# Expert-choice gathers: GpSimd waits for landed rows after every second batch instead of after each

## The chip, the cores and the metric

The kernel runs on one NeuronCore of a Trainium2 chip. The metric is the device time of one launch in microseconds (us), as the median of several runs. One further execution was taken with the hardware profiler; all rows below come from it.

## The reference

The program is an audio tower on 16 sequences of 750 steps: a convolution with batch norm, a linear-attention layer, an expert-choice mixture of experts, a cross-attention to video, and a top-2 mixture of experts. The change touches the third of these alone:

```python
affinity = softmax(einsum('bsd,de->bse', x, gate_weight)).transpose(0, 2, 1)
gating, index = top_k(affinity, k)                     # k = 92 tokens for each of 16 experts
x_in = take_along_axis(x[:, None], index[..., None], axis=2)
h = gelu(einsum('bekd,edh->bekh', x_in, w1) + b1)
x_e = einsum('bekh,ehd->bekd', h, w2) + b2
out = zeros_like(x).at[batch, index].add(gating[..., None] * x_e)
```

Each expert picks its 92 tokens of each sequence; their rows (128 numbers) are gathered, run through the expert's two layers, weighted and added back at the tokens they came from.

## The kernel before

The stage is `expert_choice_phase`. The 16 sequences are taken as 8 pairs (called p0 to p7 here). A pair has 2 x 16 x 92 picked rows, which are 23 tiles of 128 rows. The tiles are gathered in 6 batches (g0 to g5) of 4, 4, 4, 4, 4 and 3 tiles; a batch holds two tiles of each of the pair's sequences, in the order in which the experts need them.

GpSimd gathers (L1226 to L1241). For each tile it issues one indirect DMA (L1237) that reads 128 rows of `xs` in HBM, at the row numbers in a column of `rowu`, into one slot of `xg`. There is a slot for every tile of a pair, so batch g of pair p needs only that batch g of pair p-1 has been transposed (`t_ps`, L1233). Behind each batch GpSimd waits until all of its tiles have landed (L1241); each batch has a semaphore `got[g]` of its own. Before p0 and before p4 GpSimd also makes the row numbers for the next four pairs (`rows_of`, L1216), from a table `place` that ScalarE copies out of PSUM (L1289).

TensorE, ScalarE and VectorE follow one list of units that is written out ahead (`ExpertOrder.units`, L993). A unit "gathered" of batch g waits on `got[g]`, transposes its tiles on TensorE (L1389), and ScalarE copies them to `xgT` (L1301, L1303). "hidden" and "output" are the two matmuls of an expert (L1396, L1404) with ScalarE's activation behind each (L1311, L1320). "turned" transposes results back and splits them in a high part (ScalarE, L1330) and a low part (VectorE, L1183), and VectorE builds selection matrices (L1191). "spread" multiplies them into the token sums (L1428), "added" adds a sequence's sums to `h` (L1444, L1202). The front units of pair p+1 (gathered, hidden, output) are woven between the spread units of pair p, so that in p0 only front units run, and after that both kinds run together. One unit "rows" in the middle of p2's spreads (L1015) turns the lists for p4 to p7 into the table `place`.

While p0 to p2 run, VectorE also picks the tokens of the last eight sequences (L1155 to L1159).

Of the kernel before, what the change touches and what calls it, by code (L numbers as in the profile page):

```python
# [1021 lines left out]
def expert_choice_phase(nc, k):  # L1022

    stack, sb, sem = phase_scope(nc, k)
    with stack:
        F32R = mybir.dt.float32r
        HB = B // 2
        order = ExpertOrder()
# [39 lines left out]
        got = [sem(f"got{g}") for g in range(order.BATCHES)]  # L1068
# [14 lines left out]
        def column(p, tile):  # L1083
            return p * TILES + tile
# [4 lines left out]
        with nc.Block() as block:  # L1089
            @block.sync  # L1090
            def _(sp):
                sp.dma_start(base[:], k.expert_base).then_inc(tables, 16)
                sp.dma_start(iota[:], k.token_iota.partition_broadcast(P)).then_inc(tables, 16)
                for i in range(PAIRS):
                    for g in range(4):
                        b = i * 2 + g // 2
                        sp.wait_ge(nt.normed, i * 4 + (g + 1))
                        if g % 2 == 0:
                            sp.dma_start(xs_b[b, 0:GW, :].rearrange("(j p) d -> p j d", p=P),
                                         nt.xl[:, g]).then_inc(kept[g], 16)  # L1100
                        else:
                            sp.dma_start(xs_b[b, GW:GW + 2 * P, :].rearrange("(j p) d -> p j d", p=P),
                                         nt.xl[:, g, 0:2, :]).then_inc(kept[g], 16)
                            sp.dma_start(xs_b[b, T - LAST:T, :], nt.xl[0:LAST, g, 2, :]).then_inc(kept[g], 16)
                for hf in range(2):
                    sp.wait_ge(packed, hf + 1)
                    sp.dma_start(k.lists[hf].rearrange("a (p k) -> p a k", k=CAP),
                                 pack[:, hf, :, 0:CAP]).then_inc(listed_out[hf], 16)
                    sp.wait_ge(listed_out[hf], 16)
                    if hf:  # L1110
                        sp.wait_ge(row_ps, hf)
                    sp.dma_start(listed[:], k.lists[hf].rearrange("a (t s) -> t a s", s=P)).then_inc(listed_in[hf], 16)
# [101 lines left out]
            @block.gpsimd  # L1214
            def _(pool):
                def rows_of(hf):  # L1216
                    pool.wait_ge(row_moved, hf + 1)
                    if hf == 0:
                        pool.wait_ge(tables, 32)
                    nc.gpsimd.tensor_tensor(rowf[:, :], place[:, hf * HT:(hf + 1) * HT],  # L1220
                                            base[:, hf * HT:(hf + 1) * HT], ALU.add).then_inc(row_ready, 1)
                    pool.wait_ge(row_ready, 2 * hf + 1)
                    nc.gpsimd.tensor_copy(rowu[:, hf * HT:(hf + 1) * HT], rowf[:, :]).then_inc(row_ready, 1)
                    pool.wait_ge(row_ready, 2 * hf + 2)

                for p in range(PAIRS):  # L1226
                    if p % HP == 0:
                        for g in range(4):
                            pool.wait_ge(kept[g], 16 * (1 + g % 2) * (p + HP))
                        rows_of(p // HP)  # L1230
                    for g in range(order.BATCHES):
                        if p:
                            pool.wait_ge(t_ps, (p - 1) * order.BATCHES + g + 1)  # L1233
                        lows, highs = order.batch[g]
                        for j, tile in enumerate(lows + highs):
                            col = column(p, tile)
                            nc.gpsimd.indirect_dma_start(  # L1237
                                out=xg[:, 4 * g + j, :], out_offset=None, in_=k.xs,
                                in_offset=bass.IndirectOffsetOnAxis(ap=rowu[:, col:col + 1], axis=0),
                            ).then_inc(got[g], 16)  # L1240
                        pool.wait_ge(got[g], 16 * order.count(g) * (p + 1))  # L1241

            @block.scalar
            def _(act):
# [1139 lines left out]
```

## Time and profile before

| What | us |
|---|---|
| runs | 2298.33, 2295.48, 2301.55 |
| median of the runs | 2298.33 |
| the profiled execution's own time | 2295.3 |
| span of its instructions | 2293.4 |
| first gather issued (L1237) | 669.9 |
| last gather issued (L1237) | 986.1 |
| last addition to `h` in this stage (L1207) | 1033.4 |

Times in the rows are us from the start of the span; durations marked ns are not. PE is TensorE's matmuls, PEld its weight loads (which run ahead of the matmuls by a little), DVE is VectorE, ACT is ScalarE, POOL is GpSimd. A bracket at a row's end is the time that the engine was idle before it, and what released it; "issue" means that nothing in the profile shows what it waited for. PEclk is the granted TensorE clock, 1.00 being 2.4 GHz and 0.50 being 1.2 GHz.

### The profile page before, as it was taken

The page shows a single profiled execution, that of the slowest core. Times are in us where ns is not written, and L with a number is a line of the kernel's source. Part 1 is how long each engine was busy: PE and PEld are TensorE (multiplying, and loading weights), DVE is VectorE, ACT ScalarE, POOL GpSimd, SP SyncE. Part 2 cuts the span into 40 slices and gives each one's busy share as a digit, 9 for nine tenths or more (in the row PEclk, how much of TensorE's full clock was granted, in tenths as well). Part 3 has the DMA queues.
Part 4 walks back from the last instruction along what each step waited for, and adds up shares of the span by engine and source line. Part 5 has one row for each costly group of instructions (what it writes and reads, how often), then busy time and mean ns, then how long its engine had stood idle before and what let it go on. Part 6 is the DMA issues. An engine that isn't in the chain of part 4 may idle for free. (4 is left out here: it accounts for less than half of the span.)

```text
span 2293.4 us, 54841 instructions
## 1 busy us (share of the span) xinstructions
PE 2042.9 (89%) x20986; PEld 1801.0 (79%) x20986; DVE 1628.5 (71%) x4183; ACT 1075.9 (47%) x2698; POOL 608.5 (27%) x650
## 2 busy tenths in 40 slices
PE   6699999989747888986999999985999999999998
PEld 5488777778536878874777777775999999999998
DVE  4755556554583855665999999987777777777773
ACT  4433333332344555644666666642444444444443
POOL 0002222220025555511333333333212221221220
PEclk9799999999868999998999999997999999999999
DMA  8100000100211111100000000000000000000000
GB/s 184 42 1 12 11 11 11 15 8 1 76 56 40 42 34 40 41 10 2 3 3 3 3 3 3 3 2 1 8 8 14 7 7 14 7 7 14 7 8 14
DMA packets 80356, 44.52 MB, mean 19 GB/s; under 512 B 45800, under 2 KB 74024, under 8 KB 79752
## 3 DMA queue, kind: packets, MB, share of 16 engines
q1 hardware_dynamic: 74248, 29.53, 5.7%
q0 software_dynamic: 5888, 12.07, 2.0%
q8 instruction: 137, 2.24, 0.4%
q14 instruction: 83, 0.68, 0.1%
HBM read 27.20 MB, written 14.38 MB: 18 GB/s over the span
## 5 line engine op out<-in xcount | busy, mean ns | idle before, releaser
L2105 ACT ACTIVATE w<-banks,b 128x384 f32<-128x384 f32 (+1 forms) x512 | 259.7, 573 | 393.0 <-PE banks L2179 393.0
L2161 PE MATMUL banks<-w,w 128*128 128x128 f32 (+1 forms) x3072 | 364.1, 275 | 0.0
L2161 PEld LDWEIGHTS banks<-w,w 128*128 128x128 f32 (+1 forms) x3072 | 350.4, 189 | 9.1 <-issue 8.7
L1689 PE MATMUL banks<-qT,w 64*64 64x128 f32 x4608 | 272.2, 271 | 3.2 <-ACT eb L1641 2.4
L1697 PE MATMUL banks<-eb,w 64*64 64x128 f32 x4608 | 272.4, 271 | 0.2 <-DVE eb L1596 0.2
L1689 PEld LDWEIGHTS banks<-qT,w 64*64 64x64 f32 x4608 | 249.3, 133 | 16.6 <-DVE eb L1596 2.2
L1661 POOL TENSOR_TENSOR t<-eb 128x768 f32<-128x768 f32 x96 | 174.6, 1819 | 309.2 <-ACT eb L1641 299.3
L1697 PEld LDWEIGHTS banks<-eb,w 64*64 64x64 f32 x4608 | 249.2, 133 | 0.9 <-DVE eb L1596 0.8
L2002 DVE SCALAR_TENSOR_TENSOR h<-banks,t_wt,h 128x128 f32 (+3 forms) x672 | 183.8, 344 | 83.1 <-PE banks L2161 79.7
L1237 POOL DMA_INDIRECT xg<-xs,rowu x184 | 179.5, 976 | 127.0 <-DMA xg<-xs,rowu 84.7
L1596 DVE TENSOR_TENSOR eb<-eb,rd 128x1536 f32<-128x1536 f32 x96 | 208.6, 2172 | 2.1 <-ACT rd L1650 2.1
L2177 PE MATMUL banks<-t_xh,t_w1h 128*128 128x384 f32 (+1 forms) x512 | 182.5, 356 | 0.1
L1592 DVE TENSOR_REDUCE nm<-banks 128x128 bf16<-128x1536 f32 x96 | 167.8, 1748 | 10.8 <-PE banks L1689 10.8
L2179 PE MATMUL banks<-t_xh,t_w1l 128*128 128x384 f32 (+1 forms) x512 | 171.7, 335 | 0.0
L2178 PE MATMUL banks<-t_xlo,t_w1h 128*128 128x384 f32 (+1 forms) x512 | 171.0, 334 | 0.0
L2045 POOL TENSOR_TENSOR t_rstd<-t_nv,t_minus_half 128x6 f32<-128x6 f32 x48 | 63.6, 1326 | 399.7 <-DVE t_nv L1903 398.3
L1641 ACT ACTIVATE eb<-banks 128x512 f32<-128x512 f32 x288 | 150.5, 598 | 0.0
L1183 DVE SCALAR_TENSOR_TENSOR x_yl<-banks,gates,x_yh 128x128 fp32r<-128x128 f32 x184 | 52.0, 345 | 129.3 <-ACT x_yh L1330 129.1
L1428 PE MATMUL banks<-x_sel,x_yh 128*128 128x374 f32 (+1 forms) x384 | 119.7, 393 | 2.1 <-ACT x_oT L1339 1.9
L1191 DVE TENSOR_SCALAR x_sel<-iota,place 128x748 fp32r<-128x748 f32 x184 | 104.6, 622 | 6.3 <-PE banks L1428 6.2
L729 ACT ACTIVATE DT<-banks 128x768 f32<-128x768 f32 x60 | 48.7, 811 | 123.6 <-PE banks L822 123.6
L1428 PE MATMUL banks<-x_sel,x_yl 128*128 128x374 f32 (+1 forms) x384 | 98.8, 339 | 0.0
(300 smaller groups left out, 4325.3 us busy)
## 6 DMA issues: line engine op xcount, KB each, us to landing
out<-h SPq DMA_DIRECT2D x16, 320.0 KB
xs<-r_xl SPq DMA_DIRECT2D x16, 192.0 KB, 2.8
h<-in_xT SPq DMA_DIRECT2D x4, 750.0 KB, 14.8
h<-in_xT SPq DMA_DIRECT2D x4, 749.0 KB, 17.6
xg<-xs,rowu POOLq DMA_INDIRECT x184
xs<-r_xl SPq DMA_DIRECT2D x16, 128.0 KB
blocks<-NT SPq DMA_DIRECT2D x24, 48.0 KB, 1.9
D<-blocks SPq DMA_DIRECT2D x24, 48.0 KB, 2.1
```

What stands on the lines that cost most here:

```text
L1237: nc.gpsimd.indirect_dma_start(out=xg[:, 4 * g + j, :], out_offset=None, in_=k.xs, in_offset=bass.IndirectOffsetOnAxis(ap=rowu[:, col:col ...
L1428: last = nc.tensor.matmul(k.ps[:, 5 + s, 0:TW // 2], y[lo:hi, col % 8, :], sel[lo:hi, col % SEL, s * (TW // 2):(s + 1) * (TW // 2)], start ...
L1596: nc.vector.tensor_tensor(eb[:, w % 4], eb[:, w % 4], rd[:, w % 2, None, :].to_broadcast([P, FR, P]), ALU.mult).then_inc(w_ready, 1)
L1661: nc.gpsimd.tensor_tensor(t1[:, n % 2], e[:, 0:6], e[:, 6:12], ALU.add).then_inc(tree, 1)
L1689: last = nc.tensor.matmul(lbanks(n)[place(n, hd), v, :], k.Kt[half(hd), v, :], qT[half(hd), n // NC % 2, (n % NC) * P:(n % NC + 1) * P], s ...
L1697: last = nc.tensor.matmul(k.ps[half(hd), 6, 0:P], k.Vd[place(a, hd), v, half(hd)], eb[place(a, hd), a % 4, v, :], start=(v == 0), stop=(v ...
L2002: last = nc.vector.scalar_tensor_tensor(out=hh, in0=k.psf[0:n, o:o + P], scalar=wt[0:n, par, c * E1 + e:c * E1 + e + 1], in1=hh if e else ...
L2105: nc.scalar.activation(gb[u % 2][:, f, s * GW:s * GW + NFREE[s]], k.ps[:, order.bank(n), 0:NFREE[s]], ACT.Relu, bias=k.b1_1[:, 2 * e + f:2 ...
L2161: last = nc.tensor.matmul(k.psf[0:n, o:o + P], gb[u % 2][:, f, c * P:c * P + n], k.w2_1[:, 2 * e + f, :], start=(f == 0), stop=(f == 1))
L2177: nc.tensor.matmul(ps, w1h[:, 2 * e + f, :], xh[:, g, 0:w], start=True, stop=False)
L2178: nc.tensor.matmul(ps, w1h[:, 2 * e + f, :], xlo[:, g, 0:w], start=False, stop=False)
L2179: nc.tensor.matmul(ps, w1l[:, 2 * e + f, :], xh[:, g, 0:w], start=False, stop=True).then_inc(full, 1)
```

## The change

The wait of L1241 stands behind the odd batches alone, and there it waits for the even batch before it and then for the odd one. Nothing else is changed.

```diff
@@ -1238,7 +1238,9 @@
                                 out=xg[:, 4 * g + j, :], out_offset=None, in_=k.xs,
                                 in_offset=bass.IndirectOffsetOnAxis(ap=rowu[:, col:col + 1], axis=0),
                             ).then_inc(got[g], 16)
-                        pool.wait_ge(got[g], 16 * order.count(g) * (p + 1))
+                        if g % 2:
+                            for done in (g - 1, g):
+                                pool.wait_ge(got[done], 16 * order.count(done) * (p + 1))
```

On GpSimd's own program, the gathers of p0 stand like this before (`got0` to `got5` are the landings of the six batches, `row_ready` the row numbers, `g_t_ps` the transposes that free a slot):

```order
L1237 DMA xg<-xs,rowu 128x128 [waits row_ready]
L1237 DMA xg<-xs,rowu 128x128 x3
L1237 DMA xg<-xs,rowu 128x128 [waits got0]
L1237 DMA xg<-xs,rowu 128x128 x3
L1237 DMA xg<-xs,rowu 128x128 [waits got1]
L1237 DMA xg<-xs,rowu 128x128 x3
L1237 DMA xg<-xs,rowu 128x128 [waits got2]
L1237 DMA xg<-xs,rowu 128x128 x3
L1237 DMA xg<-xs,rowu 128x128 [waits got3]
L1237 DMA xg<-xs,rowu 128x128 x3
```

A wait is shown on the instruction that follows it. In the changed kernel the same place on GpSimd, and the first batches of p1 behind it, read:

```order
L1237 DMA xg<-xs,rowu 128x128 [waits row_ready]
L1237 DMA xg<-xs,rowu 128x128 x7
L1237 DMA xg<-xs,rowu 128x128 [waits got1,got0]
L1237 DMA xg<-xs,rowu 128x128 x7
L1237 DMA xg<-xs,rowu 128x128 [waits got3,got2]
L1237 DMA xg<-xs,rowu 128x128 x6
L1237 DMA xg<-xs,rowu 128x128 [waits g_t_ps,got5,got4]
L1237 DMA xg<-xs,rowu 128x128 x3
L1237 DMA xg<-xs,rowu 128x128 [waits g_t_ps]
L1237 DMA xg<-xs,rowu 128x128 x3
L1237 DMA xg<-xs,rowu 128x128 [waits g_t_ps,got1,got0]
```

The gathers are issued in runs of 8, 8 and 7 instead of 4, 4, 4, 4, 4 and 3. From p1 on, the wait for a free slot (`g_t_ps`) stays ahead of every batch. The order of instructions on the other engines is the same as before.

## Rows read from the trace of the kernel before

**Rows 1.** Waits by line, 669 to 990 us: us in total, times, longest.

```profile
POOL xg L1237 <- DMA xg<-xs,rowu: 84.7, 46, 2.4
POOL xg L1237 <- issue: 41.6, 136, 0.4
PE banks L1389 <- DMA xg<-xs,rowu: 34.5, 15, 6.7
```

**Rows 2.** Timeline of POOL: start us, us, instruction, [idle before it, releaser].

```profile
669.88 1.20 POOL L1237 DMA_INDIRECT xg<-xs,rowu  x1 [0.30 <-POOL rowu L1223]
...
676.59 0.94 POOL L1237 DMA_INDIRECT xg<-xs,rowu  x1 [1.76 <-DMA xg<-xs,rowu]
...
708.57 0.94 POOL L1237 DMA_INDIRECT xg<-xs,rowu  x1 [1.81 <-DMA xg<-xs,rowu]
...
822.67 0.94 POOL L1237 DMA_INDIRECT xg<-xs,rowu  x1 [0.31 <-issue]
833.29 0.84 POOL L1220 TENSOR_TENSOR rowf<-place,x_base 128x92 f32<-128x92 f32 x1 [9.67 <-ACT place L1289]
...
834.89 0.98 POOL L1237 DMA_INDIRECT xg<-xs,rowu  x1 [0.43 <-POOL rowu L1223]
```

**Rows 3.** Busy time by stretch: us, PE, PEld, DVE, ACT, POOL, PEclk, DMA share, GB/s.

```profile
669.00:708.50 39.50, 17.52 (x60) 12.82 (x59) 14.84 (x26) 12.34 (x32) 22.51 (x25) 0.59 0.15 39
873.50:912.00 38.50, 35.25 (x220) 32.14 (x219) 24.13 (x64) 23.61 (x70) 22.28 (x23) 1.00 0.16 40
```

**Rows 4.** Timeline of PE, transposes of gathered batches (L1389), p0, p1 and p4.

```profile
703.10 1.12 PE L1389 MATMUL banks<-ident,xg 128*128 128x128 f32 x4 [2.25 <-DMA xg<-xs,rowu]
...
720.15 0.60 PE L1389 MATMUL banks<-ident,xg 128*128 128x128 f32 x4
721.74 0.63 PE L1389 MATMUL banks<-ident,xg 128*128 128x128 f32 x4 [0.30 <-DMA xg<-xs,rowu]
728.22 1.11 PE L1389 MATMUL banks<-ident,xg 128*128 128x128 f32 x4 [3.45 <-DMA xg<-xs,rowu]
...
741.36 0.66 PE L1389 MATMUL banks<-ident,xg 128*128 128x128 f32 x4 [0.74 <-DMA xg<-xs,rowu]
...
847.93 1.11 PE L1389 MATMUL banks<-ident,xg 128*128 128x128 f32 x4 [4.75 <-DMA xg<-xs,rowu]
...
854.50 0.66 PE L1389 MATMUL banks<-ident,xg 128*128 128x128 f32 x4 [1.23 <-DMA xg<-xs,rowu]
...
861.35 0.66 PE L1389 MATMUL banks<-ident,xg 128*128 128x128 f32 x4 [2.10 <-DMA xg<-xs,rowu]
867.93 0.66 PE L1389 MATMUL banks<-ident,xg 128*128 128x128 f32 x4 [0.86 <-DMA xg<-xs,rowu]
```

**Rows 5.** Timeline of PEld, weight loads of g4's transposes (812.98: g3), p2 to p7.

```profile
780.53 0.42 PEld L1389 LDWEIGHTS banks<-ident,xg 128*128 128x128 f32 x4 [0.26 <-DMA xg<-xs,rowu]
...
812.98 0.42 PEld L1389 LDWEIGHTS banks<-ident,xg 128*128 128x128 f32 x4 [0.72 <-DMA xg<-xs,rowu]
819.95 0.42 PEld L1389 LDWEIGHTS banks<-ident,xg 128*128 128x128 f32 x4 [1.55 <-DMA xg<-xs,rowu]
...
906.40 0.42 PEld L1389 LDWEIGHTS banks<-ident,xg 128*128 128x128 f32 x4 [0.40 <-DMA xg<-xs,rowu]
...
944.79 0.42 PEld L1389 LDWEIGHTS banks<-ident,xg 128*128 128x128 f32 x4 [0.33 <-DMA xg<-xs,rowu]
...
983.34 0.42 PEld L1389 LDWEIGHTS banks<-ident,xg 128*128 128x128 f32 x4 [0.52 <-DMA xg<-xs,rowu]
```

**Rows 6.** Stretches around p1's third batch and p4's second: as Rows 3.

```profile
730.00:735.00 5.00, 5.00 (x23) 4.97 (x22) 2.99 (x9) 2.68 (x9) 2.59 (x4) 0.65 0.21 56
...
845.00:850.00 5.00, 2.07 (x8) 2.08 (x9) 0.44 (x1) 0.92 (x3) 2.58 (x4) 0.62 0.15 39
```

**Rows 7.** Durations of gathers and selections: ns min/median/max, first and last start.

```profile
L1237 POOL DMA_INDIRECT xg<-xs,rowu x184: 942/947/1340, 669.9 to 986.1; - x184
L1191 DVE TENSOR_SCALAR x_sel<-iota,place x184: 584/603/815, 709.4 to 1026.9; 128x748 fp32r<-128x748 f32 x184
```

## The prediction

> **What bounds the stage now.** I read the waits first. In this stage GpSimd is held 46 times until a batch has landed, 84.7 us in all, so 1.84 us a time; between two gathers of one batch it loses 41.6/136 = 0.31 us [rows 1]. With the bare 0.947 us of a gather [rows 7], a batch of four takes some 5 us to issue and 1.5 us more until the next begins. The waits follow each other without a pause in which GpSimd is idle for another reason, but for the change of tables at 823.6 to 834.9 us [rows 2]: GpSimd paces itself.
>
> The second view is the timeline: does anyone need the rows that soon? From the first gather of p0 (669.88) to the first of p1 (708.57) GpSimd takes 38.7 us a pair [rows 2]. TensorE is held 15 times, 34.5 us in all, by rows that have not landed [rows 1], and the reader should see where. In p0 TensorE has only front units to do and is busy 17.5 of 39.5 us at a mean clock of 0.59; in p5 it is busy 35.3 of 38.5 us at full clock [rows 3]. So the gathers bound the ramp plainly, and the steady part seems bound by TensorE. But the weight loads show that even there batch g4 is met exactly as it lands, in every pair from p2 on, with waits of 0.26 to 1.55 us [rows 5]. GpSimd's pace and TensorE's own are within half a microsecond of each other per pair. The question is therefore not how much GpSimd saves, but how far TensorE can go ahead before its own pace binds.
>
> **What one removed wait is worth on GpSimd.** Behind an even batch the 1.84 us wait becomes an ordinary gap of 0.31 us: 1.53 us each, three in a pair, 4.6 us of 38.7, 24 in all, so 36.8 us of GpSimd's time. The wait that stays should cost what it does now: the even batch was issued some 5 us before and has landed, so the first of the two waits passes at once. I take the landing itself as unchanged, because the wait behind the last batch of p0, which has three gathers, is 1.81 us, and behind the first, which has four, 1.76 us [rows 2]: nothing piles up. At one gather per 1.25 us, and landed some 1.5 us after its issue, no more than two are in flight, with the wait or without.
>
> So a batch lands earlier by 1.53 us for each even batch between it and the last fixed start. The fixed starts are 669.88 (p0) and, for p4 to p7, the table `place`.
>
> **p0 and p1.** Batch g4 of p0 has two fewer waits ahead of it: TensorE transposes it at 703.10 - 3.06 = 700.04. From there to g0 of p1 it waits for no rows, 17.05 us (703.10 to 720.15 [rows 4]); so 717.1. For g1 it was held 0.30 us and will not be: 718.4. It is ready for g2 3.03 us later (728.22 - 3.45 - 721.74), at 721.4; g2 now has four fewer waits ahead and lands at 728.22 - 6.1 = 722.1. TensorE is still held, by 0.7 us instead of 3.45. From g2 to g4 it needs 741.36 - 0.74 - 728.22 = 12.40 us, part of it at the lowered clock that followed the 3.45 us pause (0.65 in 730 to 735 [rows 6]); without the pause some 1 us less, my estimate from that clock over half of those 5 us. So it is ready for g4 at 733.5 to 734.5, and g4 lands at 741.36 - 5 x 1.53 = 733.7. The gain up to here is 6.9 to 7.65 us; I take **7.3**. The landing caps it: if TensorE's clock rose sooner in p0, it would meet g2 and g4 of p1 at the same times.
>
> **p2 and p3.** Here GpSimd is ahead for good (at g4 of p3, 11 waits or 16.8 us earlier against TensorE's 9). What is left to gain is the waits for rows that end: 0.26, 0.72 and 1.55 us on the weight loads [rows 5], 2.5 us; on the matmuls less shows, so **2.2**. From then on TensorE runs at its own pace, and GpSimd's saving buys nothing.
>
> **The change of tables.** GpSimd finishes p3 12 waits (18.4 us) earlier, but `place` comes from the unit "rows" on TensorE, which moves only by 9.5 us. The idle time ahead of L1220, 9.67 us [rows 2], grows to some 18.6 us: the larger part of what GpSimd saved in p0 to p3 becomes this wait. No other engine waits on GpSimd here.
>
> **p4.** Gathers start anew from the table, and TensorE has nothing left to run ahead of. It was held 4.75 us for g1, 1.23 for g2, 2.10 for g3, 0.86 for g4 [rows 4]. Counted from the table, g1 and g2 land 1.53 us earlier, g3 and g4 3.06. Between the batches TensorE needs 5.34, 4.75 and 5.72 us (start to start, less the waits). So g2 would be ready at 847.93 - 1.53 + 5.34 = 851.74 and lands at 852.97; g3 is ready at 857.72 and lands at 858.29; g4 is ready at 864.01 and lands at 864.87. It is held to the end by rows, so g4 gains the whole **3.06**. If the clock stays low longer (0.62 in 845 to 850 [rows 6]), less: with 1 us more between g3 and g4, 2.9.
>
> **p5 to p7.** With GpSimd ahead again, the waits for g4 end: 0.40 + 0.33 + 0.52 = **1.25 us** [rows 5]. Slots are no limit: at the first gather of p7 GpSimd is ahead by 9 more waits, 13.8 us, on a lead of nearly a pair.
>
> **Sum.** 7.3 + 2.2 + 3.06 + 1.25 = 13.8 us. The profiled execution takes 2295.3 us, of which 1.9 lies around the span; it would take 2281.5. The median of the runs is 2298.33, 3.0 above it, and they spread over 6 us; I carry the gain over to the median: **2284.5 us**. What follows the stage starts when its last addition is done and moves with it. The bounds of the terms (6.9 to 7.65, 1.7 to 2.5, 2.0 to 3.06, 0 to 1.25) give 10.6 to 14.5 us, 2283.8 to 2287.7; with the spread of the runs, 3 us to each side, about 2280.5 to 2291.
>
> **A rule that speaks against it.** The rows say that a gather takes 947 ns as a median, 1340 at most, while VectorE makes 184 selections of 603 ns beside them, and a pair's 23 gathers take 22.3 us on GpSimd against a bare 23 x 0.947 = 21.8 [rows 3, 7]: at most half a microsecond a pair is lost to whatever VectorE does. The Trainium skill, page "SBUF — State Buffer", section "SBUF: two separate sides", says that while VectorE runs a fast-mode operation GpSimd is locked out of their common port and cannot write a DMA's descriptors. By that rule alone each selection could hold a gather for its whole 603 ns, 13.9 us a pair as an estimate, three times what the change saves; the trace shows half a microsecond, and I go by the trace.
>
> **The rivals.**
>
> *TensorE's own pace binds sooner.* Only the waits of the two ramps count: g4 of p0 gains 3.06 us, and p4 gains 3.06; in p1 the chain of ScalarE and TensorE, or a clock that comes up later, takes the rest. For it: p5 looks full (35.3 busy of 38.5 [rows 3]). Against it: TensorE is idle 3.45 us for g2 of p1 [rows 4], and that wait has four fewer ahead of it. 6.1 us, 2292.2 us: no change by the measure below. Chance 0.11.
>
> *An even batch lands only with the odd one behind it.* Then the gathers between two waits act as one: g4 of p0 comes with g5, three gathers of 1.25 us later, at 703.8 instead of 700.04, later than now; g4 of p1 at 733.7 + 3.75 = 737.5, a gain of 3.9; p2 and p3 still give 2.2; in p4, g4 comes at 864.87 + 3.75 = 868.6 and loses 0.7. That leaves 5.4 us: 2292.9. The equal waits behind three and four gathers speak against it [rows 2]. Chance 0.05.
>
> *Slower: gathers stretch.* Denser gathers meet VectorE's selections more often, and each is issued more slowly. The point from which this decides is 4.6/23 = 0.2 us a gather, a mean of 1.15 us. The longest seen is 1.340 us [rows 7], 0.39 above the median: 9.0 us a pair if all were like that, 4.4 worse than now, and over 8 pairs 35 us, 2333 us. It would strike all pairs, since GpSimd would again set the pace of each. Half a microsecond a pair now speaks against it. Chance 0.05. The page named above stands behind this rival.
>
> **How the numbers follow.** The forecast has 0.79. A difference of over 0.3%, 6.9 us here, is about what a measurement of this kernel tells from no change: faster means below 2291.4. The forecast's range lies there, but a draw of runs can take 0.01 of it out, and the first rival's 2292.2 can fall on either side (0.03 of its 0.11): 0.81 faster. Same: 0.08 of the first rival, the second's 0.05 and the forecast's 0.01, 0.14. Slower: the third, 0.05. The range for 8 in 10 goes from 2279 to 2293, to take in the first rival.
>
> **What would show it.** Right: 22 waits of some 1.84 us ahead of gathers on GpSimd instead of 46; g4 of p1 transposed near 734 and never met at its landing from p2 to p3 and from p5 on; the wait ahead of the second L1220 near 18.6 us; TensorE's waits for rows down from 34.5 us to about 23, nearly all in p0 and p4. Wrong: gathers with a mean above 1.1 us, waits for rows in p5 to p7, or a wait of 3 us or more left at g2 of p1.

## The result, and the profile after

The changed kernel takes 2337.64 us in the median, the kernel before 2297.49 in the runs beside it: a ratio of 1.0178, 95% interval 1.0161 to 1.0195. Slower by 40 us; the forecast was 2284.5. The profiled execution's span is 2335.6 us.

Where does the time go? The first gather is issued at 669.81, as before; the last addition to `h` of this stage comes at 1075.3 instead of 1033.4. So nearly the whole loss, 41.9 us of the 42.2 between the two profiled spans, arises in this stage. I look first at what the forecast spoke of. GpSimd's timeline in the changed kernel (start us, us, instruction, idle before it and releaser):

```profile
669.81 1.20 POOL L1237 DMA_INDIRECT xg<-xs,rowu  x1 [0.30 <-POOL rowu L1223]
...
682.11 0.94 POOL L1237 DMA_INDIRECT xg<-xs,rowu  x1 [2.37 <-DMA xg<-xs,rowu]
...
694.01 0.94 POOL L1237 DMA_INDIRECT xg<-xs,rowu  x1 [2.23 <-issue]
...
704.76 0.94 POOL L1237 DMA_INDIRECT xg<-xs,rowu  x1 [2.33 <-issue]
...
847.70 0.37 POOL L1220 TENSOR_TENSOR rowf<-place,x_base 128x92 f32<-128x92 f32 x1 [37.22 <-ACT place L1291]
```

Against [rows 2] p0 is issued in 34.9 us instead of 38.7: GpSimd did get ahead. Each wait that stays is 2.2 to 2.4 us instead of 1.84. And the wait for the table `place` is 37.2 us, where 18.6 was forecast. The page's group of gathers and TensorE's transposes (the same view as [rows 4]) say that the rows came early:

```profile
L1237 POOL DMA_INDIRECT xg<-xs,rowu x184 | 179.1, 973 | 114.6 <-issue 86.3
```

```profile
700.43 0.95 PE L1391 MATMUL banks<-ident,xg 128*128 128x128 f32 x4 [2.07 <-DMA xg<-xs,rowu]
706.54 0.49 PE L1391 MATMUL banks<-ident,xg 128*128 128x128 f32 x3
721.38 1.05 PE L1391 MATMUL banks<-ident,xg 128*128 128x128 f32 x4
723.48 1.05 PE L1391 MATMUL banks<-ident,xg 128*128 128x128 f32 x4
728.19 0.60 PE L1391 MATMUL banks<-ident,xg 128*128 128x128 f32 x4
732.42 0.60 PE L1391 MATMUL banks<-ident,xg 128*128 128x128 f32 x4
740.90 0.60 PE L1391 MATMUL banks<-ident,xg 128*128 128x128 f32 x4
```

A gather's issue has a mean of 973 ns: nothing stretched. Batch g4 of p0 is transposed at 700.43 (forecast 700.04). But p1 begins at 721.38, later than the 720.15 of before, and from there to p4 TensorE waits for rows no more: it is late by itself. Seven of the waits of 669 to 1005 us (us in total, times, longest) name the new cause:

```profile
ACT x_yT L1322 <- remote: 20.9, 9, 5.3
PE banks L1406 <- ACT x_yT L1322: 19.8, 12, 4.9
POOL xg L1237 <- PE banks L1391: 20.5, 5, 12.2
ACT hid L1313 <- remote: 18.9, 10, 4.1
PE banks L1391 <- DMA xg<-xs,rowu: 17.6, 6, 7.1
PE banks L1398 <- ACT hid L1313: 13.1, 11, 2.4
DVE x_sel L1191 <- remote: 8.4, 5, 2.4
```

TensorE's row waits fell from 34.5 us [rows 1] to 17.6. "Remote" is new: before has no such wait in the stage. Here ScalarE is held by a semaphore of TensorE whose matmul had long ended by the profile. One place in p1, first ScalarE, then TensorE, then GpSimd beside them:

```profile
786.93 0.41 ACT L1322 ACTIVATE x_yT<-banks,b 128x184 f32<-128x184 f32 x1 [3.21 <-remote]
```

```profile
781.09 0.48 PE L1406 MATMUL banks<-hid,w 128*128 128x184 f32 x2
...
782.12 0.47 PE L1398 MATMUL banks<-xgT,w 128*128 128x184 f32 x2
787.49 0.95 PE L1406 MATMUL banks<-hid,w 128*128 128x184 f32 x2 [4.90 <-ACT x_yT L1322]
```

```profile
775.48 0.94 POOL L1237 DMA_INDIRECT xg<-xs,rowu  x1 [2.35 <-PE banks L1391]
...
784.22 0.94 POOL L1237 DMA_INDIRECT xg<-xs,rowu  x1 [0.30 <-issue]
787.40 1.01 POOL L1237 DMA_INDIRECT xg<-xs,rowu  x1 [2.24 <-issue]
```

The output matmul (L1406) ends at 781.57, and TensorE goes on to others; ScalarE, which needs its result, starts at 786.93. A semaphore update is the mark that a finished instruction sets for the engines that wait for it; the trace holds the times of these events. They tell what came between (time of the event, and how long after the end of the latest matmul that can have made it):

```
782.56  TensorE L1416   2.59
785.42  TensorE L1430   3.14
786.87  TensorE L1446   5.61
786.91  TensorE L1406   5.34
786.97  TensorE L1430   4.69
787.01  TensorE L1398   4.42
```

Four updates of TensorE come out within 0.15 us, in the break between a run of eight gathers and the next. A matmul's end is modelled in these profiles (the Trainium skill, page "Perfetto Trace Analysis", section "Tensor Engine Instruction (MATMUL, LD_WEIGHTS)", says so too), but an error of the model would not end for four matmuls at once. I call an update late when it comes over 0.4 us after the latest matmul that makes it. Of the events that the trace holds from 690 to 1000 us (it lacks some: 465 stand there for 531 matmuls that make one in before, 373 for 445 in the changed kernel), 36 of TensorE's 465 are late in before, 25.6 us in all; in the changed kernel 111 of 373, 225.7 us. VectorE and ScalarE have none late in either, and after the last gather TensorE has none either.

What late updates cost shows where TensorE does the same work. The next rows (columns as in [rows 3]) go from the last batch's transposes of one pair to those of the next: first before, p1 to p2, then the changed kernel, p1 to p2 and p2 to p3.

```profile
748.91:788.10 39.19, 35.22 (x219) 32.20 (x218) 33.99 (x85) 23.38 (x69) 22.73 (x24) 1.00 0.16 42
```

```profile
748.86:805.87 57.01, 41.52 (x219) 37.68 (x218) 34.47 (x85) 23.59 (x71) 34.84 (x37) 0.88 0.18 47
805.87:841.92 36.05, 34.51 (x219) 32.24 (x218) 23.27 (x65) 23.42 (x70) 3.24 (x3) 1.00 0.03 7
```

The same 219 matmuls take 57.0 us instead of 39.2 while GpSimd is at work on 37 gathers beside them, and 30 of the 57 updates on record are late. TensorE is idle 11.5 us more, and its matmuls take 6.3 us more at a mean clock of 0.88 instead of 1.00. In the next stretch GpSimd issues its last gathers before the table and then waits for it (3 instead of 37 fall in the stretch); no update is late, and TensorE needs 36.05 us, less than before's 39.4 for that pair. Up to the last batch of p1 the two kernels are level (748.86 and 748.91); the loss arises in p2 (17.8 us), p5 (19.4) and p6 (12.6). In p3 and p7, with 3 gathers each in these stretches, it gains 3.4 and 2.8 on before, and in p4, where TensorE has rows to wait for, 1.7.

### The profile page after: what moved, and what is told of

The parts are those of the page before. It is cut to its first block and busy times, and to the rows that moved or that the text cites. A ratio compares the mean times of both kernels' runs of the same rounds, so it can differ in the third digit from the quotient of the medians.

```text
span 2335.6 us, 54823 instructions
## 1 busy us (share of the span) xinstructions
PE 2064.0 (88%) x20986; PEld 1819.6 (78%) x20986; DVE 1628.5 (70%) x4183; ACT 1075.2 (46%) x2698; POOL 607.2 (26%) x650
## 5 line engine op out<-in xcount | busy, mean ns | idle before, releaser
L1430 PE MATMUL banks<-x_sel,x_yh 128*128 128x374 f32 (+1 forms) x384 | 125.0, 408 | 3.7 <-ACT x_oT L1341 2.9
L1191 DVE TENSOR_SCALAR x_sel<-iota,place 128x748 fp32r<-128x748 f32 x184 | 105.3, 622 | 19.4 <-PE banks L1430 11.0
L1430 PE MATMUL banks<-x_sel,x_yl 128*128 128x374 f32 (+1 forms) x384 | 104.3, 355 | 0.0
```

The source lines that it names most:

```text
L1430: last = nc.tensor.matmul(k.ps[:, 5 + s, 0:TW // 2], y[lo:hi, col % 8, :], sel[lo:hi, col % SEL, s * (TW // 2):(s + 1) * (TW // 2)], start ...
```

## The experiments

The theory: TensorE's semaphore updates are held up while GpSimd issues gathers closely, and the longer the run, the longer. Rivals: it is the landing that must be awaited; the second wait instruction costs the time; the bytes or the rows of the gathers do it; TensorE's updates are too many. Unless a diff shows more, it replaces the wait of L1241, `pool.wait_ge(got[g], ...)`. "Landed" stands for that line. `pause(n)` is n memsets on GpSimd, each waited for:

```diff
+        idle, idled = sb("x_idle", [P, 400]), sem("x_idled")
...
+                def pause(times):
+                    for _ in range(times):
+                        nc.gpsimd.memset(idle[:], 0.0).then_inc(idled, 1)
+                        pauses[0] += 1
+                        pool.wait_ge(idled, pauses[0])
```

### A pause in place of the landing

```diff
+                        if g % 2:
+                            wait for landed g - 1, then g
+                        else:
+                            pause(3)
```

> The changed kernel, but behind each even batch GpSimd clears a scratch tile three times (some 1.5 us by its other clears) without waiting for any row. Theory 'pause': TensorE's semaphore updates queue up while GpSimd issues gathers back to back, from the fourth in a row on, and any stretch without a gather lets them through; then runs of four come back and the time returns to that of before, 2290 to 2303 us. Theory 'landing': the updates queue until GpSimd has waited for its rows, so that what counts is the number of gathers since the last such wait; then the time stays at 2330 to 2345 us, as in the changed kernel (2337.6).

Measured: 2309.19 us, ratio 1.0053 (1.0034 to 1.0072); 41 of 411 late. Nothing is awaited behind an even batch, and 28 of the 40 us are back. The time lies above the 2290 to 2303 expected; the rest goes with GpSimd's pace, whose runs of four start 6.94 us apart (median of p0 to p3) instead of 6.61. e8 below has the same 6.94 and takes 2307.15 us.

### Runs of twelve

```diff
+                        if g % 3 == 2:
+                            wait for landed g - 2, g - 1, then g
```

> The wait stands behind every third batch (12 and 11 gathers in a row). If the loss grows with the length of the run (both theories above): TensorE's updates come later still, and the time lies above the changed kernel's 2337.6, at 2345 to 2380 us. Rival, a fixed price of having more than one batch in flight: within 5 us of 2337.6, 2333 to 2343.

Measured: 2356.22 us, ratio 1.0263 (1.0236 to 1.0290); 86 of 342 late, 276.6 us. The loss grows with the run.

### The second wait instruction, alone and left out

Before with one wait more (e8), and the change with one wait less (e9):

```diff
 e8
+                        wait for landed g - 1 (odd g only), then g
 e9
+                        if g % 2:
+                            wait for landed g
```

> Before, with one more wait for the even batch's rows ahead of the odd batch's own, which are long satisfied when GpSimd comes to it. Theory (a second wait instruction costs GpSimd some 0.4 us, as the odd waits of 2.2 to 2.4 us against 1.84 suggest): three such waits a pair, 1.2 us a pair and up to 9.6 us in all where GpSimd paces; with TensorE's own pace in p2, p3 and p5 to p7 part of it hidden: 2300 to 2307 us. Rival (a satisfied wait is free, the longer wait comes from the eight gathers): 2297 us, odd waits of 1.84 us.

> The changed kernel with only the odd batch's own wait behind it: runs of eight gathers, one wait. Theory that the loss comes from the runs of eight: 2328 to 2338 us, late updates of TensorE as in the changed kernel, odd waits near 1.84 us. Rival that the second wait brings a large part of the loss: under 2315 us.

Measured: e8 2307.15 us, ratio 1.0046 (1.0029 to 1.0062); e9 2340.43, ratio 1.0193 (1.0176 to 1.0210). Two rows of GpSimd's timeline in e8, behind the first even and the first odd batch:

```profile
677.10 0.94 POOL L1237 DMA_INDIRECT xg<-xs,rowu  x1 [1.70 <-DMA xg<-xs,rowu]
...
684.05 0.95 POOL L1237 DMA_INDIRECT xg<-xs,rowu  x1 [2.25 <-DMA xg<-xs,rowu]
```

A wait that is already satisfied is not free on GpSimd: 0.55 us here, 0.48 between the medians of the odd and the even batches. 24 of them are 13 us at most, and e8 is 10 us slower: most of it shows in the time, so in before a delay of GpSimd is passed on nearly whole. But in the changed kernel this is not the loss: e9 without it is as slow.

### The change in p0 alone

```diff
+                        if g % 2 or p:
+                            wait for landed g - 1 (odd g only), then g
```

> The even waits are gone in the first pair alone, where TensorE has little to do and is held by the rows themselves; all other pairs wait behind each batch as before. By the prediction's own terms this first pair gives 3 to 4.6 us; where the late updates cost as much there as elsewhere (40 us over 8 pairs, 5 a pair), it is lost again. Theory 'late updates': 2293 to 2303, no gain beyond 3 us. Rival, the prediction's sum holds where GpSimd is the bound: 2290 to 2294.

Measured: 2301.27 us, ratio 1.0024 (1.0009 to 1.0040). This edit puts the second wait into every pair, so it is to be read against e8, which has it too: p0's earlier rows are worth 5.9 us.

### A short pause behind each batch, and one twice as long

```diff
 e4, memset of 400 elements
+                        pause(1)
 e6, memsets of 300 elements
+                        pause(2)
```

> No wait for landed rows on GpSimd at all; behind each batch of four it clears a scratch tile once (some 0.45 us, with the gaps around it 0.8 us without a gather instead of 1.84). Theory 'pause', if the queued updates drain in well under a microsecond (in the changed kernel's trace they come out 0.05 us apart): GpSimd runs ahead, TensorE is not held, 2280 to 2292 us. If draining takes the whole 1.8 us or begins only once the last gather has landed (1.25 us behind its issue): as bad as the changed kernel or worse, 2335 to 2380.

> No wait for landed rows at all; behind every batch GpSimd does two short memsets instead, a gap of some 1.4 us between batches where before shows 1.84. Theory (TensorE's semaphore updates get out only when GpSimd stops issuing gathers for about 1 us): a gap of 1.4 us is enough, late updates stay as few as in before, and GpSimd takes some 35 to 36 us a pair instead of 38.7; the ramps of p0, p1 and p4 gain: 2283 to 2292 us. Rival (it is the landing that must be awaited, or more than 1.8 us without a gather): as many late updates as with runs of eight, 2320 us or more.

Measured: e4 2372.30 us, ratio 1.0337 (1.0294 to 1.0380), 105 of 369 late, 324.3 us; e6 2296.72, ratio 1.0013 (0.9994 to 1.0032), 65 of 435 late, 61.6 us. Neither waits for a landing at all. e4's batches start 5.49 us apart (median of p0 to p3), e6's 6.03; the longer pause is nearly enough, though the gain expected of it did not come.

### More updates on TensorE

```diff
+                                if y is yh or s == 0:
+                                    last.then_inc(extra, 1)
```

(at the spread matmuls, L1428; the wait of L1241 stays)

> Before, with 72 more semaphore updates a pair on TensorE (three of four spread matmuls that gave none now add 1 to a semaphore nobody waits for). Theory that TensorE's updates stand in one queue that is drained slowly, about one per 0.74 us, while gathers are issued: the queue gets longer and the updates that ScalarE and VectorE wait for come later: 2320 us or more. Rival (an update is held for as long as the run of gathers lasts, however many there are, and all held ones come out together in the pause): 2297 us within 5.

Measured: 2297.20 us, ratio 1.0001 (0.9991 to 1.0012). The theory of a queue drained one by one falls. Around 780 ten held updates, eight of them of spread matmuls, come out within 0.33 us. They are 0.03 to 0.05 us apart, while such matmuls start 0.17 us or more apart: TensorE had gone on running them, and what waited was their updates.

### Half the bytes, half the rows

Both with e9's single wait, and with `xg` set to zero ahead (e12 takes each half row at half the row's address):

```diff
 e12
-                                out=xg[:, 4 * g + j, :], out_offset=None, in_=k.xs,
+                                out=xg[:, 4 * g + j, 0:C // 2], out_offset=None, in_=k.xs.rearrange("r (h c) -> (r h) c", h=2),
 e13
+                                out=xg[0:P // 2, 4 * g + j, :], out_offset=None, in_=k.xs,
+                                in_offset=bass.IndirectOffsetOnAxis(ap=rowu[0:P // 2, col:col + 1], axis=0),
```

> Runs of eight with the odd batch's own wait alone; each gather fetches 128 rows of half the length (256 bytes instead of 512), the other half of each row is left as zeros, so that part of the computation is left out. If it is the bytes that the gathers move which keep TensorE's updates back: late updates fall to before's share, under 2315 us. If it is the descriptors or the issue: 2332 to 2343 us, as with whole rows.

> Runs of eight with the odd batch's own wait alone; each gather fetches only the first 64 of its 128 rows, the other 64 are left as zeros, so that part of the computation is left out. If the number of rows (descriptors) decides: GpSimd's issue gets shorter or the late updates fall to before's share, under 2315 us. If each gather instruction does it whatever it fetches: 2332 to 2343 us.

Measured: e12 2349.86 us, ratio 1.0231 (1.0209 to 1.0253); e13 2370.17, ratio 1.0337 (1.0308 to 1.0365). Neither bytes nor rows decide it. Both lie above the 2332 to 2343 us that this would give and are slower than e9; that the gathers come closer still, as what follows makes likely, was not tested apart. e12's runs of eight start 11.49 us apart (median of p0 to p3) where e9's start 11.72 apart, and in e13 a gather follows in 1.21 us.

### The distance of the gathers

By now I could measure how long the hold lasts. From the first gather of an uninterrupted run to the last late update that comes behind it (median of the runs that have one):

| run of | kernel | us | us a gather |
|---|---|---|---|
| 4 | before | 5.72 | 1.43 |
| 7 | changed | 10.08 | 1.44 |
| 8 | changed | 11.47 | 1.43 |
| 12 | e2 | 17.17 | 1.43 |

As if each gather took 1.43 us of something that TensorE's updates need, while the next follows in 1.25. By this e4, whose batches need 5.72 us and get 5.49, falls further behind with each. Five kernels with no break and no landing wait at all, only a memset behind each gather, differ in its length alone (300, 210, 100, 50 and 8 elements):

```diff
                             ).then_inc(got[g], 16)
+                            pause(1)
-                        pool.wait_ge(got[g], 16 * order.count(g) * (p + 1))
```

> No wait for landed rows and no break between batches: GpSimd does one short memset behind every gather instead, so that gathers start some 1.65 us apart throughout, 38 us a pair as in before. Theory that each gather keeps TensorE's updates back a little longer than the 1.25 us to the next one (the burst of late updates comes 0.95 us after the issue of the last of four gathers, some 1.75 us after that of eight, so 0.2 us more a gather), and the rest adds up: at 1.65 us nothing adds up, few late updates at any place, 2285 to 2300 us. Rival (updates get out only in a break of about 1 us between gathers): there is none, late updates everywhere, 2340 us or more.

> As the run with a memset behind every gather, with a shorter memset: gathers start some 1.48 us apart instead of 1.6, 34 us a pair instead of 38.7 in before. Theory of a fixed hold: each gather keeps TensorE's updates back for 1.43 us (the last late updates come 5.7 us after the start of an uninterrupted run of four gathers, 11.5 us after that of eight, 17.2 us after that of twelve), one after the other; at 1.48 us apart nothing adds up, so hardly any late updates, and GpSimd is as fast as the change wanted it: the gain forecast for the change comes, 2283 to 2290 us. Rival (any denser issue makes updates late, the 1.6 us were merely long enough by far): late updates throughout, 2305 us or more.

> The same with gathers some 1.37 us apart, 31.5 us a pair. Theory of a fixed hold of 1.43 us: 0.06 us adds up with every gather and there is no break in which it could be made up, over 1 us after one pair and about 4 us before the next table, so late updates nearly throughout, 2300 to 2330 us, slower than with 1.48 although GpSimd is faster. Rival (what counts is GpSimd's pace): faster than with 1.48.

> The same with 50 elements, starts some 1.38 us apart. Theory of a fixed hold: between the two, a little slower than 1.42 or the same, 2278 to 2300 us. Rival (another instruction in between is enough): faster than 2280 us.

> A memset of only 8 elements behind every gather: starts some 1.33 us apart where nothing holds GpSimd, against 1.42 in the run before this one that was fastest (2280.0 us). Theory of a fixed hold of 1.43 us: 0.1 us adds up with every gather, two to three times a pair's worth more than with 1.42, and late updates become the rule as they are in runs of eight: slower than 2280, 2290 to 2330 us. Rival (it is enough that some other instruction of GpSimd stands between two gathers): no more late updates than with 1.42, 2275 to 2282 us.

Measured, by the median distance of the gathers' starts:

| run | distance, us | late, of | late in all, us | time, us | ratio (95%) |
|---|---|---|---|---|---|
| e5 | 1.585 | 0 of 405 | 0 | 2302.48 | 1.0023 (1.0013 to 1.0032) |
| e14 | 1.510 | 0 of 420 | 0 | 2287.24 | 0.9960 (0.9945 to 0.9975) |
| e15 | 1.417 | 48 of 422 | 49.2 | 2280.00 | 0.9927 (0.9907 to 0.9947) |
| e18 | 1.380 | 109 of 384 | 181.8 | 2343.81 | 1.0195 (1.0176 to 1.0215) |
| e17 | 1.344 | 121 of 361 | 261.3 | 2363.47 | 1.0272 (1.0235 to 1.0310) |

The time falls with the distance down to about 1.43 us, and 0.04 us less costs some 60 us, each run against before beside it (e18's five runs lie 2329 to 2357 us; the profiled one is the fastest). So it is the distance, not the break, and not that some other instruction stands in between. e17 and e18 came out slower than either side of their forecasts. e5 and e14 have no "remote" wait at all in the stage; below 1.43 us they are back, as these three of the waits of e17 (669 to 1005 us) show:

```profile
ACT x_yT L1329 <- remote: 29.2, 17, 3.8
ACT hid L1320 <- remote: 21.0, 10, 3.4
ACT x_yh L1339 <- remote: 16.6, 7, 5.9
```

For e15 I had expected 2300 or more and was wrong: the memset came out longer than planned, and the mean distance in p0 to p3 is 1.50 us, over the hold, since some memsets are longer than others. The mean does not settle it, however: e18 has 1.47 us without its three waits for free slots, also over the hold. What tells them apart is how far the gathers fall behind. Counting 1.43 us for each gather from its start or from the end of the one before, whichever is later, the arrears reach 0.30 us at most in e15, 1.35 in e18, 3.54 in e17 and 1.27 in the changed kernel, and are nothing in e5 and e14. Two rows of e15's GpSimd timeline:

```profile
805.91 0.20 POOL L1221 MEMSET x_idle<- 128x100 f32 x1
...
807.54 0.51 POOL L1221 MEMSET x_idle<- 128x100 f32 x1
```

41 of its 184 memsets take some 0.49 instead of 0.20 us. Each of the 41 begins while a selection of VectorE (L1192) runs and ends 0.11 to 0.12 us after it; the ten that begin before a selection, or within 0.08 us of its start, take 0.20. That agrees with the Trainium skill, page "SBUF — State Buffer", section "SBUF: two separate sides", by which a fast-mode operation of VectorE shuts GpSimd out of their common port. Whether the selection is such an operation, no row tells. Here it only gave the updates time.

### Versions

Runs of eight where TensorE has little else to do, p0 and p4 (e11); the same, and a memset of 210 elements behind each gather in all other pairs (e16):

```diff
 e11
+                        if g % 2 or p % HP:
+                            wait for landed g
 e16
+                            if p % HP:
+                                pause(1)
+                        if g % 2 and p % HP == 0:
+                            wait for landed g
```

> The change in p0 and p4 only, with the odd batch's own wait alone behind it; all other pairs as in before. In p0 and in p4 TensorE waits for rows and has little else to do, so late updates should cost it less than the earlier rows bring. Theory: p0 gains what the run with the first pair alone showed against the run with the second wait alone, 2307.2 - 2301.3 = 5.9 us, p4 up to 3 us: 2288 to 2292 us. Rival (late updates eat it there too): 2297 us or more.

> Runs of eight gathers with the odd batch's own wait in p0 and p4, where TensorE waits for rows; gathers 1.48 us apart and no wait in all other pairs. Theory: about what 1.48 us everywhere gives, or up to 4 us less, since the first batches of p0 and p4 land about 1 us earlier each: 2279 to 2288 us. Rival (a backlog of late updates left by p0 and p4 lasts into p1 and p5): slower than 1.48 us everywhere.

Measured: e11 2287.81 us, ratio 0.9964 (0.9950 to 0.9977); e16 2284.78, ratio 0.9951 (0.9933 to 0.9968). Both beat the two kernels, and e11 needs no memset. In p0 and p4 the earlier rows are worth more than the late updates cost. e16 is no faster than e14 by more than their runs spread. The fastest of all is e15.

## Why the prediction was wrong

**GpSimd's side held.** It was to take 38.7 - 4.6 = 34.1 us a pair and took 34.9 to 35.4 in p0 to p2; the 0.8 to 1.3 us above it is "the first of the two waits passes at once", which took some 0.5 us three times a pair. "I take the landing itself as unchanged" held: g4 of p0 came at 700.43 against 700.04. TensorE's waits for rows fell, to 17.6 us where about 23 was forecast, all of it in p0 and p4.

**The step that failed** stands in p0 and p1: "From there to g0 of p1 it waits for no rows, 17.05 us". It waited for no rows and took 20.95 us (700.43 to 721.38), as these stretches of before and of the changed kernel show:

```profile
703.10:720.15 17.05, 13.82 (x60) 10.51 (x61) 4.94 (x11) 10.37 (x30) 10.59 (x11) 0.81 0.15 39
```

```profile
700.43:721.38 20.95, 14.90 (x60) 11.09 (x61) 5.08 (x11) 10.72 (x32) 13.03 (x14) 0.75 0.17 44
```

For the same 60 matmuls TensorE is idle 2.8 us longer, and busy 1.1 longer at a lower mean clock. Five updates are late there, by 0.54 to 1.70 us, where before has none. The term 7.3 rests on it, and so do all that follow, by "From then on TensorE runs at its own pace": I took TensorE's pace from before as its own, one that knows nothing of GpSimd's. It was a pace under gathers in runs of four, whose hold of 5.72 us ends before the next run starts at 6.61; the changed kernel's runs of eight hold it for 11.47 us. The sum has no term for this. "Nothing piles up" was read from the landings alone, and before's trace held the sign that something does: 36 late updates, all of matmuls that ended after the third gather of a run had begun, in semaphore events that I did not read.

**Without most of the hold the sum comes out in total, not term by term.** e15 is another kernel, but it brings the rows earlier by about the same (32.8 to 35.8 us a pair), with 49.2 us of late updates instead of 225.7. Its transposes g2 and g4 of p1:

```profile
721.60 1.01 PE L1398 MATMUL banks<-ident,xg 128*128 128x128 f32 x4 [1.76 <-DMA xg<-xs,rowu]
...
735.97 0.60 PE L1398 MATMUL banks<-ident,xg 128*128 128x128 f32 x4
```

The forecast had g2 held until 722.1 and g4 near 734. Its wait for `place` is 18.82 us (forecast 18.6), and its last addition comes at 1020.2, 13.2 us earlier than before's 1033.4 (forecast 13.8). But at g4 of p1 it is 5.4 us ahead of before, where 7.3 was forecast, and it still gains 3.3 us from g4 of p4 to g4 of p7 (971.32 against 983.34), where 1.25 was: before, at 38.4 to 38.6 us a pair there, did not run at TensorE's own pace, which was 36.05 in the changed kernel's pair almost without gathers. That the total agrees is in part luck.

**The change of tables and p4.** The wait of 37.2 instead of 18.6 us comes from the unit "rows" on TensorE, which is late with the rest. "Slots are no limit" failed too: GpSimd got so far ahead of a slow TensorE that it waited five times for a transposed batch, 20.5 us.

**The rivals.** "Slower: gathers stretch" gave 2333 us, close to the result, but by a mechanism that did not occur: it needed a mean of 1.15 us, and it is 0.973. (The "half a microsecond a pair" against it was p5's; before's mean of 0.976 us makes it 0.7 over all pairs.) The other two did not occur either. None of the three had TensorE held by what GpSimd issues.

## What to carry to other kernels

A wait that seems to guard nothing may be what spaces an engine's DMA issues; before removing it, find out what else the gap gives time to, and try the bare gap (a pause without the wait) beside the removal. If indirect gathers on GpSimd run beside matmuls whose results others wait for, keep their starts at a measured distance (here 1.43 us; a median of 1.42 was 17 us faster than before, 1.38 was 43 us slower), and spread it evenly rather than in bursts with a long wait. In a profile, hold an engine's semaphore updates against the ends of its instructions; a wait on "remote" is the place to look.

## What the runs showed of the hardware

- Gathers that GpSimd issues less than 1.43 us apart keep TensorE's semaphore updates back, although the issue of one takes 0.94. The last of them come out some 1.43 us a gather after the start of the run: 5.72 us after four, 11.47 after eight, 17.17 after twelve. Gathers 1.51 us apart or more hold nothing: no update of e14 or e5 comes more than 0.02 us after its matmul. Only TensorE's updates are held: VectorE and ScalarE have no late one in any of the runs shown. The hold depends neither on the bytes (e12) nor on the rows (e13: 11.48 us after eight in the median, 7.9 to 12.2), nor on the number of updates (e7). What the gathers occupy was not shown, nor whether other DMAs of GpSimd do the same. Nor why updates made during the first two gathers of a run are on time (0 of 194 late in before), while of the later ones some are late and some not: 36 of 271 in before, and 101 of the 156 made from the fifth gather of a run on in the changed kernel.
- A satisfied wait on GpSimd costs some 0.5 us (e8: 2.25 against 1.70 us).
- A memset of GpSimd that begins during a selection of VectorE ends 0.11 to 0.12 us after it: 0.49 us instead of 0.20 (e15, 41 times).
